# Key transposes of a cross-attention moved from TensorE to VectorE blocks and DRAM, and a reordered attention-only turn

## The reference

```python
q = x @ Wq.T                       # 32 heads of 16
k = context @ Wk_part.T            # 361 rows a batch, 32 heads of 16
q, k = rmsnorm(q), rmsnorm(k)      # over the 16 channels of a head
scores = einsum('bhnd,bhmd->bhnm', q, k) * 16 ** -0.5
out = einsum('bhnm,bhmd->bhnd', softmax(scores), v)
```

## Time and profile before

| | |
|---|---|
| runs (3) | median 1312.95 us, 1312.74 to 1315.94 |
| profiled execution | 1312.68 us, its span 1310.9 us |
| TensorE busy | 1268.3 us, 97% of the span |
| VectorE, ScalarE, GpSimd busy | 781.7, 648.9, 295.8 us |
| DMA | 63.98 MB, mean 49 GB/s |

### The profile page before, as it was taken

The page is one execution under the profiler, slowest core; times in us unless marked ns, Lnnn a source line. Parts: engine busy times, 40 slices in busy tenths (PEclk is TensorE's granted clock), DMA queues, the critical chain, the costliest instruction groups (busy, mean ns, idle before and its releaser), DMA issues.

```text
span 1310.9 us, 27154 instructions
## 1 busy us (share of the span) xinstructions
PE 1268.3 (97%) x10784; PEld 850.2 (65%) x10784; DVE 781.7 (60%) x1890; ACT 648.9 (50%) x1524; POOL 295.8 (23%) x293
## 2 busy tenths in 40 slices
PE   8989999999999999999999999999999999999998
PEld 7656666666666666566666666666666665666554
DVE  6897788777877787434344434554455784443423
ACT  4663344343433356377777776666665523232221
POOL 0564454334334451111101101111101121000000
PEclk9999999999999999999999999999999999999999
DMA  8102000000000021112222222001012310000000
GB/s 330 73 9 73 9 8 10 7 3 9 9 8 9 9 88 63 72 32 84 105 73 73 74 73 89 25 25 58 25 58 84 125 52 24 1 24 1 24 1 30
DMA packets 18744, 63.98 MB, mean 49 GB/s; under 512 B 1850, under 2 KB 3386, under 8 KB 15418
## 3 DMA queue, kind: packets, MB, share of 16 engines
q1 hardware_dynamic: 18618, 62.24, 13.4%
HBM read 55.68 MB, written 3.28 MB: 45 GB/s over the span
## 4 chain that ended last, share of the span: by engine, by line
PE 83%; DVE 6%; issue 5%; ACT 4%; POOL 2%; DMA 0%; POOLq 0%; SPq 0%; DVEq 0%; ACTq 0%
PE A L1861 18%; PE A L1761 11%; PE C L2214 10%; PE A L1824 10%; PE C L1892 6%; PE B L1912 4%; PE C L1789 3%; PE A L2233 3%; PE A L1842 3%; PE B L2233 2%; PE C L1806 2%; PE A L1770 2%; PE B L1781 2%; PE B L1878 1%; PE B L1797 1%
## 5 line engine op out<-in xcount | busy, mean ns | idle before, releaser
L1861 PE MATMUL A<-wxhl,arena 128*126 128x512 f16 x1104 | 254.7, 381 | 3.2 <-DVE arena L1221 2.6
L1861 PEld LDWEIGHTS A<-wxhl,arena 128*126 128x126 f16 x1104 | 145.4, 136 | 86.3 <-issue 8.1
L1761 PE MATMUL A<-arena,wxhl 128*125 128x512 f16 (+1 forms) x780 | 174.5, 380 | 1.3 <-DVE tub L1140 1.3
L855 ACT ACTIVATE arena<-C 126x1600 f32<-126x1600 f32 x96 | 144.4, 1504 | 22.3 <-PE C L1892 22.3
L595 POOL TENSOR_TENSOR arena<-arena,region 126x512 f32<-126x512 f32 (+2 forms) x59 | 60.9, 1062 | 405.8 <-DVE region L1282 405.8
L1761 PEld LDWEIGHTS A<-arena,wxhl 128*125 128x125 f16 (+1 forms) x780 | 103.5, 136 | 62.1 <-DVE tub L1140 5.3
L2214 PE MATMUL C<-arena 128*128 128x375 f16 (+1 forms) x768 | 138.8, 333 | 0.0
L758 ACT ACTIVATE region<-C,negm 100x100 f32<-100x100 f32 x256 | 84.3, 358 | 100.8 <-DVE negm L1183 100.8
L569 POOL TENSOR_TENSOR region<-tub 125x512 f32<-125x512 f32 (+1 forms) x65 | 82.5, 1269 | 219.3 <-DVE tub L1140 217.0
L1824 PE MATMUL A<-arena,stageb 128*125 128x512 f16 (+1 forms) x416 | 124.0, 379 | 2.1 <-ACT qk L829 1.3
L2214 PEld LDWEIGHTS C<-arena 128*128 128x128 bf16 x768 | 74.8, 97 | 58.8
(11 more groups left out here) (201 smaller groups left out, 2256.5 us busy)
## 6 DMA issues: line engine op xcount, KB each, us to landing
stageb<-in_wffn SPq DMA_DIRECT2D x16, 768.0 KB, 4.8
arena<-in_ctxt SPq DMA_DIRECT2D x16, 756.0 KB, 5.8
stageb<-in_wffn SPq DMA_DIRECT2D x8, 1024.0 KB, 6.2
arena<-in_wqkv SPq DMA_DIRECT2D x4, 1024.0 KB, 12.1
wxhl<-in_wffn SPq DMA_DIRECT2D x4, 1024.0 KB, 4.7
arena<-in_wx SPq DMA_DIRECT2D x3, 1024.0 KB, 8.4
out_x<-xres SPq DMA_DIRECT2D x12, 224.0 KB
xres<-in_wo SPq DMA_DIRECT2D x2, 1024.0 KB, 19.3
```

Of the source, the lines that this page charges most:

```text
L855: act.activation(e[:, at:at + 2].rearrange("p f (r s) -> p r f s", r=RT), Call[0:KC, :].rearrange("p (r x) -> p r x", r=RT)[:, :, 0:4 * S] ...
L1761: ins = pe.matmul(A[j % 2][0:m, :], xp[:, k, at:at + m], wp[:, j, k, :], start=(n == 0), stop=(n == 11))
L1861: ins = pe.matmul(A[(par + n) % 2][0:KC, :], xp[:, k, c * KC:(c + 1) * KC], wp[:, 1 if n < 4 else 2, k, :], start=(i == 0), stop=(i == 11))
```

## The change

Group 0 of the keys is turned as before, and for batch 0 all groups are. For the batches 1 to 15, groups 1 to 3 go another way. VectorE transposes 32x32 blocks of a key tile's 384 channels (`turn_keys`, one instruction a tile) into `kts`. SyncE writes each tile to DRAM in four transfers, one for each band of 32 partitions, in runs of 32 elements (128 bytes), so that the blocks come to lie in their transposed places (`keys_out`). It waits until the writes of tiles 0 and 1 have landed, reads both back into `kTd` with one transfer, and then reads tile 2 (`keys_in`). The rows shared with the next batch are read once more in the next turn (`keys_shared`). `scores2(b, 1)` waits for the first read, `scores2(b, 2)` for the others. ScalarE's copies of these groups go, and VectorE's `turn_keys` stand in its turn as shown, with `x2_lo` moved ahead of them and, in turn 14, the statistics behind them.

In the turns that only attend, the first z transpose moves ahead of the output projection and the others one place forward, the first transpose of weights goes in ahead of the projection's last three matmuls, and the third uses the bank A[1] instead of B[1], so that it does not wait for VectorE. VectorE takes the fifth z group ahead of the attention sum.

```diff
-        kT = carve([128, 2, NT, CTXP])
+        kT0 = carve([128, 2, CTXP])
+        kTd = carve([128, 2, NT - 1, NC * KP])
...
+        kts = carve([128, NC, KW])
...
+        kd01 = nc.dram_tensor("keys01", (2, 128, NT - 1, 2, KP), F32).ap()
+        kd2 = nc.dram_tensor("keys2", (2, 128, NT - 1, KP), F32).ap()
...
+            def keys_out(b, c):
+
+                sp.wait_ge(*count("d_kt", b, c + 1))
+                for n in range(4):
+                    block = slice(32 * n, 32 * n + 32)
+                    if c < 2:
+                        dst = kd01[b % 2].rearrange("(r j) t c n -> c j t r n", r=4)[c][:, :, :, block]
+                    else:
+                        dst = kd2[b % 2].rearrange("(r j) t n -> j t r n", r=4)[:, :, :, block]
+                    sp.dma_start(dst, kts[block, c].rearrange("j (t r i) -> j t r i", t=NT - 1, r=4)).then_inc(kw[c], 16)
+
+            def keys_in(b):
+
+                for c in range(2 if short(b) else NC):
+                    keys_out(b, c)
+                sp.wait_ge(*written(0, b))
+                sp.wait_ge(*written(1, b))
+                sp.wait_ge(*count("pe_sc", b - 2, NU))
+                sp.dma_start(kTd[:, b % 2, :, 0:2 * KP], kd01[b % 2].rearrange("p t c n -> p t (c n)")).then_inc(kr01, 16)
+                if not short(b):
+                    sp.wait_ge(*written(2, b))
+                    own = own_rows(b)
+                    sp.dma_start(kTd[:, b % 2, :, 2 * KP:2 * KP + own], kd2[b % 2][:, :, 0:own]).then_inc(kr2, 16)
...
             for b in range(NB - 2):
                 if b < NB // 2:
                     sixteenth(2 * b, 0)
+                if b > 0:
+                    keys_shared(b)
+                if b < NB // 2:
                     sixteenth(2 * b + 1, 1)
                 context(b + 2)
+                keys_in(b + 1)
...
+            def turn_keys(b, c, par):
+
+                dve.wait_ge(*count("g_kn", b, c + 1))
+                dve.wait_ge(*written(c, b - 1))
+                dve.transpose(kts[:, c], raw[par][:, c, 128:512])\
+                   .then_inc(sig["d_kt"], 2 if c == 1 and short(b) else 1)
...
-                    add_attn(o_tile(b), A[0])
                     back(b, 4)
+                    add_attn(o_tile(b), A[0])
...
+                if x2_tile(b) is not None:
+                    x2_lo(x2_tile(b), B[0])
+                if end < 2:
+                    turn_keys(b + 1, 0, odd)
+                    turn_keys(b + 1, 1, odd)
                 if end == 1:
                     dve.wait_ge(*count("d_x2out", unit_tiles(0)[-1], 2))
                     row_stats3(0, range(len(unit_tiles(0))))
 
-                if x2_tile(b) is not None:
-                    x2_lo(x2_tile(b), B[0])
                 if o2_tile(b) is not None:
                     add_cross(o2_tile(b), 0)
+                if end < 2 and not short(b + 1):
+                    turn_keys(b + 1, 2, odd)
...
+                def last_heads():
+                    pe.wait_ge(*count("d_zT", i, 3))
+                    heads_back(b, 4)
+
+                def first_weights():
+                    pe.wait_ge(*count("d_zT", i, 4))
+                    p_turn(b, 0, B[1])
+
+                between(0)
                 pe.wait_ge(*count("d_u", i, 5))
-                project_out(o, b, A[0], between, late)
-                pe.wait_ge(*count("d_zT", i, 3))
-                heads_back(b, 4)
-                pe.wait_ge(*count("d_zT", i, 4))
-                p_turn(b, 0, B[1])
+                project_out(o, b, A[0], lambda g: between(g + 1), {14: last_heads, 15: first_weights})
                 pe.wait_ge(*count("d_zT", i, 5))
                 p_turn(b, 1, B[0])
+                if x is not None:
+                    pe.wait_ge(*count("d_xlo", x, 1))
+                p_turn(b, 2, A[1])
                 attend(b, 0)
                 pe.wait_ge(*count("d_pT", b, 1))
-                p_turn(b, 2, B[1])
+                p_turn(b, 3, B[1])
                 attend(b, 1)
-                pe.wait_ge(*count("d_pT", b, 2))
-                p_turn(b, 3, B[0])
```

More of the change, by code:

```diff
@@ L27 @@
 KC = 126
+KP = 128
+KW = 3 * 128
 NC = 3
@@ L260, in build @@
         carve = carver()
-        raw = [carve([KC, 4, 512]) for _ in range(2)]
+        raw = [carve([128, 4, 512]) for _ in range(2)]
         ctxs = carve([128, KT, CTXP])
@@ L435, in build, with written, own_landed @@
         g_ones = sem("g_ones")
+        pe_T0, a_T0 = sem("pe_T0"), sem("a_T0")
+        kw = [sem(f"kw{c}") for c in range(NC)]
+        kr01, kr2, krx = sem("kr01"), sem("kr2"), sem("krx")
+        def written(c, b):
+            return kw[c], 4 * 16 * sum(c < 2 or not short(n) for n in range(1, b + 1))
+        def own_landed(b):
+            return kr2, 16 * sum(not short(n) for n in range(1, b + 1))
         d_warm, a_ws, g_wlo, a_z = sem("d_warm"), sem("a_ws"), sem("g_wlo"), sem("a_z")
@@ L914, in turn @@
                     x_hi(x_tile(b), A[1])
-                flip = 0 if new else 1
-                p_back(b, 0, B[flip])
-                p_back(b, 1, B[1 - flip])
+                banks = B + B if new else [B[1], B[0], A[1], B[1]]
+                p_back(b, 0, banks[0])
+                p_back(b, 1, banks[1])
                 if new:
                     square(*new[4])
-                p_back(b, 2, B[flip])
-                p_back(b, 3, B[1 - flip])
+                p_back(b, 2, banks[2])
+                p_back(b, 3, banks[3])
                 for g in range(4):
@@ L1809, in attend, with project_out @@
                 ins.then_inc(sig["pe_av"], 1)
-            def project_out(i, b, bank, between=None, late=None):
+            def project_out(i, b, bank, between=None, late={}):
                 m, at, n = rows_of(i), i % 2 * TW, 0
@@ L1820, in project_out @@
                     for h in range(4 * g, 4 * g + 4):
-                        if late and h == 14:
-                            late()
+                        if h in late:
+                            late[h]()
                         for ap, part in ((ah, 0), (ah, 1), (al, 0)):
@@ L1884, in scores2 @@
                     pe.wait_ge(*count("d_qT", last_tile(b), 1))
+                elif b == 0 and u != 2 and u < 5:
+                    pe.wait_ge(a_T0, {1: 1, 3: 2, 4: 3}[u])
+                elif b > 0 and u == 1:
+                    pe.wait_ge(kr01, 16 * b)
+                elif b > 0 and u == 2:
+                    pe.wait_ge(*own_landed(b))
+                    if b == 1:
+                        pe.wait_ge(a_T0, 3)
+                    else:
+                        pe.wait_ge(krx, 16 * (b - 1))
                 if u > 0:
@@ L1891, in scores2 @@
                     for r in range(RT):
-                        ins = pe.matmul(C[r][0:KC, f * 2 * S:(f + 1) * 2 * S],
-                                        kT[32 * r:32 * r + 32, b % 2, t, c * KC:(c + 1) * KC],
-                                        qms[b % 2][32 * r:32 * r + 32, t].rearrange("p f s -> p (f s)"), start=True, stop=True)
+                        group = slice(32 * r, 32 * r + 32)
+                        keys = kTd[group, b % 2, t - 1, c * KP:c * KP + KC] if t else kT0[group, b % 2, c * KC:(c + 1) * KC]
+                        ins = pe.matmul(C[r][0:KC, f * 2 * S:(f + 1) * 2 * S], keys,
+                                        qms[b % 2][group, t].rearrange("p f s -> p (f s)"), start=True, stop=True)
                 ins.then_inc(sig["pe_sc"], 1)
```

84 lines of the change are left out of this document (50 added, 34 removed).

## The result

The changed kernel takes **1323.16 us** (median of 6 runs, 1320.76 to 1328.04), the kernel before 1313.95 us in the same series (6 runs, 1312.57 to 1315.94): a ratio of 1.0072, 95% interval 1.0052 to 1.0092. It is 9 us slower, where 1309 us were forecast. The time lies in the range and on the other side of no change. The profiled execution took 1323.39 us, 10.7 us more than that of before.

A forecast was written before the change was run, and what follows sets the result against it. TensorE was taken to bound the kernel, DMA costing nothing. -13.3 + 5.2 + 1.6 + 2.4 = -4.1 us against the profiled 1312.68 gave 1308.6, with 0.3 for the median 1309 us; whole range 1298 to 1334.

The forecast's parts named there:

- transposes off TensorE: Second stage: 45 groups of key transposes leave TensorE, seven of them paying nothing; -13.3 us.
- VectorE's insertions: Second stage: block transposes of 0.47 us delay VectorE's half sum in turns 2, 7, 12, 13 and 14; +5.2 us.
- keys late: Second stage: TensorE's waits at the second scores for keys coming through DRAM, summed over the turns; +1.6 us.
- turns that only attend: First stage: new wait for GpSimd before the first z transpose, partly repaid at the turn's end; 0.8 us each, +2.4 us.
- t = 0.65: Assumed us per SyncE write transfer of 128 B runs, set by issue, from a span of 0.60 to 0.80.
- 6.2 + 12t: Us from the start of GpSimd's norms until the keys are there, after 12 writes at t us each and a 3.5 us read.
- long landed: SyncE's wait before the first read: writes of tiles 0 and 1 taken as already landed, if t is the pace.
- the keys come too late: Rival at the second scores: 12 transfers slower than 0.70 us each; 1322 us at 0.80, 1338 at 0.90; chance 0.27.
- sign of a slow pace: SyncE's new issues: expected at 0.6 to 0.7 us, with no gap within a tile.
- its other sign: TensorE's waits for DMA at `scores2`: under 2 us in all, 9 us or more if the keys are late.
- Small runs are not dear: Rival on the DMA engines: 128 B runs cost 51 ns like large ones, 1.28 us a transfer; 1402 us; chance 0.07.
- both insertions are free: Rival: VectorE's half sum is not late and the turns that only attend save 4.1 us; 1297 to 1302 us; chance 0.21.

The follow-up runs named there:

- kernel without transposes and transfers: Changed kernel with batch 0's keys for groups 1 to 3 in every batch, and no VectorE key transposes, DRAM writes or reads; 1304.74 us.
- keys awaited or not: Changed kernel, but groups 1 to 3 always take batch 0's keys and nobody waits for the reads, all transposes and transfers kept; 1310.25 us.
- first stage alone: Kernel before with only the changed order in the three turns that only attend; 1318.13 us, ratio 1.0035.
- first read early: Changed kernel with the old first stage, and SyncE reading tiles 0 and 1 behind their eight writes, before tile 2's writes; 1313.45 us.
- tile by tile: Changed kernel with the old first stage, tile 0 read alone behind eight writes, tiles 1 and 2 each alone behind tile 2's writes; 1307.12 us.

## Why the prediction was wrong

Its four terms, with what the runs gave for each:

| term | predicted | measured | from |
|---|---|---|---|
| transposes off TensorE | -13.3 | -13.4 | what the others leave of the kernel without transposes and transfers |
| VectorE's insertions | +5.2 | +5.5 | transposes and transfers left out or not |
| keys late | +1.6 | +12.9 | keys awaited or not |
| turns that only attend | +2.4 | +5.1 | first stage alone |

The measured terms add up to the whole by the way they were worked out, so their sum proves nothing; each is good to 1 to 3 us, by the spread of its runs.

**The step that failed is the third.** "I take +1.6 us" was read off at a pace of t = 0.65, and the pace was right (0.66). But the step had one unknown in its chain, 6.2 + 12t, and took the rest as fixed. Three small things were each off to the same side: the read lands in 4.0 us for 3.5, the block transposes take 0.58 for 0.47, and issues in the thirteenth place, at times already ahead of it, are held up, by 0.5 to 2.0 us in each of the seven turns that waits follow. The prediction had found that the slack of most turns is used up at t = 0.65, so most of it came out in waits. The hold-ups are the largest part: all seven waits stand behind a row of issues that was held up, and none behind the rows of turns 1, 2, 3, 6 and 8, which were not. (Those of turns 7, 12 and 14 were held up too, without a wait behind them.) Taking each hold-up off the wait behind it, 1.96 us in turn 0, 1.14 in turn 13 and at most 0.9 in the five others, leaves 4.0 of the 10.1 us, by estimate.

A fourth link was left out: the writes were taken as "long landed" by the time of the read, but in turn 13, with eight, SyncE waited 1.50 us for the last, ahead of the longest wait of all.

By the prediction's own scale 1.0 us spread over 12 transfers is t = 0.73, where it has the waits pass 7 us: the mechanism of its first rival, "the keys come too late", at the point from which that rival decides. The rival put it down to a slow pace, or to an outstanding write that holds up the next. The first is refuted, the second fits the hold-ups, but what holds an issue up stays open: the trace shows that it happens, not why. The prediction's sign of a slow pace, issues outside 0.6 to 0.7 us, would have passed in most turns and missed it; its other sign, 9 us or more of waits at `scores2`, is what came.

**What a wait costs** can be more than its length. The keys' 10.1 us were worth 12 to 13. One loss of 1.7 us of clock stands behind the wait of 993.51 in the profiled execution. Whether the clock falls differs between executions: between 72 and 92 us, in turns that are the same in every kernel, it did in some profiled executions and not in others. The kernel with the first read early took 1309.41 us at a mean clock of 1.000 and 1315.94 at 0.990; that its waits were the same in both is likely and not shown, since only the first was profiled. The prediction gave the clock no price. The kernel before gave little cause to: its TensorE waits for nothing that long in the second stage, and behind 2.10 us at 80 its clock stayed at 1.00.

**The first stage** was followed on correctly up to the wait ("TensorE waits 2.1 us there", measured 2.04), and then the prediction let its gain at the end of the turn pay most of it back. Those waits go only in part: of 0.66, 0.19 and 0.53 us 0.58 and 0.19 stay. In turns 9 and 14 the turn grew by 1.09 and 1.18 us for the predicted 0.8, and in turn 4 by 2.77, because the clock fell behind the wait. Of the 2.7 us by which the term was too small 1.7 are clock by the profiled execution, the rest some 0.3 us in each turn.

**The transposes and VectorE** came out as worked: 13.4 and 5.5 us. For VectorE the waits bear it out place by place. TensorE waited 0.34 us for the half sum in turns 2, 7 and 12 (0.45 foreseen), 1.27 in turn 13 (1.0 foreseen; the row of line 1959), and in turn 9, which was not foreseen, 0.57. Turn 14 is read best where no clock fell, in the kernel with the first read early (line 1953 is `turn_queries`, 1960 `turn_heads`):

```profile
1003.70 0.56 PE L1953 MATMUL B<-cst,arena 100*128 100x100 f32 x4 [2.10 <-DVE region L1455]
...
1008.32 0.54 PE L1960 MATMUL B<-cst,arena 126*128 126x126 f32 x3 [1.47 <-DVE region L1367]
```

That is 3.57 us in place of 1.04, 2.5 more where 2.8 were foreseen, and 5.4 in all.

**The other rivals.** Small runs are not dear: with every run at the price of a large one the keys' waits would be 95 us. "DMA: Bandwidth & Descriptors", section Specifications, in the Trainium skill puts transfers under 512 B below line rate, with a read-modify-write; in this trace 384 runs of 128 B land 2.1 us behind their issue and follow each other every 0.66 us, the pace of the issue, so the rule doesn't decide here. That both insertions are free fell with the 5.5 us, and the gain of the first stage with its loss of 5.1.

## What to carry to other kernels

When a step moves from an engine to a chain of transfers, the moment to reckon with is that of the last landing against the first need, tile by tile. Issue first what the first consumer needs, in a transfer of its own, and put every other transfer behind it: here that turned a loss of 6 us into a gain of 6, with the same bytes moved. If a chain's slack comes out at about nothing, price its cost by the sum of all its uncertain links, not by the one with the largest factor. And an order that runs work early on an in-order engine needs its input to be there: the order with one z group ahead of the projection was 9 us slower than the one without.

## What the runs showed of the hardware

- A 32 x 32 block transpose of 128 x 384 float32 on VectorE takes 577 ns.
- 48 KB in 384 runs of 128 B to DRAM: 0.57 to 0.62 us of SyncE's issue, 2.1 us to landing. 192 KB back in runs of 512 B: 3.0 us; 384 KB in runs of 1 KB: 3.8 to 4.0.
- In the kernel with the first read early, eight such issues in a row keep their pace of 0.66 us save in turns 0, 13 and 14 (5.6 to 6.4 us for 5.26); in longer rows one or another takes 1.0 to 1.8 us. A read in the ninth place issued in 0.56 or 0.57 us in all 15 turns, with a pause of 1.5 us ahead of it (first read early) and without one (tile by tile). Why issues are held up stays open.
- Behind a wait of 2 to 3 us TensorE's granted clock fell to 0.50 to 0.60 for about 3 us in some cases (2.04, 3.08 and 2.12 us) and not in others (2.04 us in turn 9; 3.18 in the kernel with the first read early, whose mean clock was 1.000). In the changed kernel each fall lost 1.7 us; in other kernels some lost 3.4.
